# A routed four-layer transformer kernel: the router one gated step earlier, eight places for expert weights, and the last one-hots in a ring in another buffer

## The reference

```python
x = layernorm(x + lightning_attention(x))      # 4 x 512 tokens, 512 wide
x = layernorm(x + int8_ffn(x))
# gated layer
q, k, v = x@Wq.T+bq, x@Wk.T+bk, x@Wv.T+bv;  g = sigmoid(x@Wg.T+bg)
x = layernorm(x + q * cumsum(k*v, axis=1) * g)
# mixture of experts: 32 experts, inner width 192
p = softmax(x @ gate.T);  top8, idx = top_k(p, 8);  w = top8 / sum(top8)
prim, sec = idx[:, :4], idx[:, 4:]
best_sim, best = max over prim of similarity[sec, prim]
new_sec = where(best_sim < 0.5, sec, best)     # a second choice joins a first one
combine = sum(one_hot([prim, new_sec]) * w)
y = sum over experts of (silu(x@wg.T) * (x@wu.T)) @ wd.T * combine[:, e]
x = layernorm(x + y)
```

## Time and profile before

| | |
|---|---|
| median of 3 runs | 1631.88 us (1629.71 to 1634.39) |
| the profiled execution | 1634.86 us, its span 1633.0 us, granted clock 0.953 |
| PE / DVE / ACT / POOL busy | 90% / 58% / 44% / 47% |
| chain that ended last | PE 61%, DVE 12%, DMA 10%, issue 7%, POOL 6% |
| gated layer, 16 steps | 673.9 to about 868.8 us |
| tail of the router | about 868.8 to 970.3 us |
| expert blocks | 970.3 to about 1590 us |

### The profile page before, as it was taken

How to read it: one execution, slowest core, us unless ns; L and a number is a source line. 1 busy time by engine, 2 the same in 40 slices (tenths; PEclk the granted TensorE clock), 3 DMA queues, 4 the chain that set the end, 5 groups by cost and what they waited for, 6 DMA issues and landing times.

```text
span 1633.0 us, 33299 instructions
## 1 busy us (share of the span) xinstructions
PE 1462.1 (90%) x11189; PEld 825.5 (51%) x11190; DVE 944.4 (58%) x1869; ACT 724.8 (44%) x1311; POOL 770.8 (47%) x699
## 2 busy tenths in 40 slices
PE   3899999999999999999996369998988999999980
PEld 1566666644444444445553226664545666666650
DVE  6777777776757576624879664443333444444435
ACT  5344433555464546434554334443333444444443
POOL 2455554530010101233566255565555887776745
PEclk9999999999999999999997579999999999999995
DMA  6233111279677777511111058999998999888869
GB/s 234 60 122 101 29 32 33 77 246 314 225 257 229 257 234 257 180 50 52 54 54 52 2 192 222 256 277 250 268 239 242 168 169 166 152 145 143 149 94 315
DMA packets 97102, 269.52 MB, mean 165 GB/s; under 512 B 15152, under 2 KB 15568, under 8 KB 91920
## 3 DMA queue, kind: packets, MB, share of 16 engines
q1 hardware_dynamic: 61424, 182.75, 33.5%
q0 software_dynamic: 35616, 85.99, 27.0%
HBM read 158.83 MB, written 101.47 MB: 159 GB/s over the span
## 4 chain that ended last, share of the span: by engine, by line
PE 61%; DVE 12%; DMA 10%; issue 7%; POOL 6%; ACT 2%; SPq 1%; DVEq 0%; POOLq 0%; ACTq 0%
PE bank L866 15%; PE bank L546 10%; PE bank L887 8%; DMA acc<-X,WA 7%; PE bank L678 6%; PE bank L684 6%; PE bank L707 6%; PE bank L857 4%; DMA XT<-x_rows,WA 2%; DVE ARENA L1009 1%; POOL ARENA L1637 1%; POOL ARENA L1642 1%; PE bank L876 1%; ACT ARENA L1357 1%; PE bank L787 1%
## 5 line engine op out<-in xcount | busy, mean ns | idle before, releaser
L866 PE MATMUL bank<-ARENA,XT 128*128 x1908 | 367.2, 329 | 2.5 <-issue 1.4
L1768 POOL DMA_INDIRECT acc<-X,WA x159 | 252.7, 1590 | 140.7 <-DMA acc<-X,WA 65.9
L866 PEld LDWEIGHTS bank<-ARENA,XT 128*128 128x128 f16 x1908 | 181.2, 98 | 127.9 <-issue 14.8
L1321 DVE COPY XT<-bank 128x1024 f16<-128x1024 f16 x159 | 110.0, 692 | 213.0 <-PE bank L857 191.7
L887 PE MATMUL bank<-ARENA,XT 128*128 x795 | 200.2, 383 | 0.7 <-issue 0.5
L1357 ACT ACTIVATE ARENA<-ARENA 128x512 f16<-128x512 f32 (+2 forms) x128 | 89.3, 709 | 248.2 <-DVE ARENA L1093 133.3
L1762 POOL DMA_INDIRECT XT<-x_rows,WA x159 | 156.9, 987 | 83.4 <-DVE XT L1331 45.4
L1596 ACT ACTIVATE XT<-bank 128x192 f32<-128x192 f32 x159 | 52.5, 330 | 310.0 <-PE bank L866 260.9
L546 PE MATMUL bank<-WA,XT 128*128 128x512 f16 (+1 forms) x768 | 137.4, 333 | 24.1 <-DVE WA L929 19.8
L546 PE MATMUL bank<-XT,STG 128*128 128x512 f16 x640 | 150.7, 383 | 0.0
L1357 ACT ACTIVATE XT<-bank 128x384 f16<-128x384 f16 (+2 forms) x207 | 125.8, 608 | 31.7 <-PE bank L535 22.2
(11 more groups left out here) (218 smaller groups left out, 2389.0 us busy)
## 6 DMA issues: line engine op xcount, KB each, us to landing
w_scratch<-WA SPq DMA_DIRECT2D x64, 640.0 KB, 3.9
ARENA<-w_scratch SPq DMA_DIRECT2D x32, 1280.0 KB
ARENA<-w_exp SPq DMA_DIRECT2D x48, 640.0 KB, 5.3
WA<-w_exp SPq DMA_DIRECT2D x16, 640.0 KB, 5.2
ARENA<-ARENA SPq DMA_DIRECT2D x64, 128.0 KB, 2.3
acc<-ARENA SPq DMA_DIRECT2D x18, 256.0 KB, 3.0
x_rows<-ARENA SPq DMA_DIRECT2D x17, 256.0 KB, 2.4
STG<-xT SPq DMA_DIRECT2D x8, 512.0 KB, 4.3
```

What stands on the lines that cost most here:

```text
L866: mm = pe.matmul(d, xTb[k.u % 2][:, a * KD + kd, :], weights(sl, b, kd * 2 * DFF, 2 * DFF), start=(a, b, kd) == (0, 0, 0), stop=(a, b, kd) ...
L1321: dve.tensor_copy(xTb[k.u % 2].rearrange("p c n -> p (c n)"), bank[k.u % 2][:, :].bitcast(F16)).then_inc(xt_sb, 1)
L1768: pool.indirect_dma_start(acc[i % 2], bass.IndirectOffsetOnAxis(blkidx[:, i:i + 1], 0), yD[i % 8], None, compute_op=ALU.add).then_inc(y_ou ...
```

## The change

- Each router piece in the gated layer moves to an earlier place: `logits(b)` and `choices(b)` from the fourth to the third step of the batch after, `second_choices`, `similarities` and `combine` from the two steps behind that into the fourth step, `ranks` and `places` one step forward, and `slot_sums` to the end of the fourth step of batch b + 2. With this `second_choices(2)`, `similarities(2)` and `slot_sums(1)` leave the tail.
- `combine` is split: its first eight instructions are now `candidates`. In the tail `candidates(2)` runs ahead of the last residual and norms; 12 of the 32 value one-hots of batch 2 run between `choices(3)` and `candidates(3)`, and their slot sums before `ranks(3)`.
- POOL makes its row one-hots ahead of the step's product, and its `shifts` behind it for q >= 2.
- The one-hots of batches 2 and 3 lie in STG, where the weights of the gated layer were, in a ring of 19. Before, batch 2 used 32 places beside batches 0 and 1, and batch 3 a ring of 12.
- `Wslot` has eight places. The first load waits only for `slot_sums(1)`; loads 1 to 3 follow behind the rows of batch 3; places 4 to 7 lie over the gated layer's buffers and wait until these are read. From the ninth on a load waits for the expert eight before.

```diff
@@ -39,6 +39,6 @@
 NBLK = TOK * TOPK // P + EXPERTS - 1
-NSLOT = 4
+NSLOT = 8
 NG = 8
 AHEAD = 2
-NLAST = 12
+NLAST = 19
 WCOLS = KD * 2 * DFF + 2 * DIM
@@ -178,3 +178,3 @@
 
-        r = Region(ARENA, NSLOT * 4 * WCOLS)
+        r = Region(ARENA, 4 * 4 * WCOLS)
         kC, qC, gC, kvC, cumC, a1C, onesC = (r.take([SEQ], F32) for _ in range(7))
@@ -190,7 +190,7 @@
         r = Region(ARENA)
-        oneR = [[r.take([P], F16) for _ in range(ROWS_B)]] * 3
-        oneV = [[r.take([4 * P], F16) for _ in range(ROWS_B)]] * 3
-        r = Region(ARENA, NSLOT * 4 * WCOLS)
-        oneR.append([r.take([P], F16) for _ in range(NLAST)])
-        oneV.append([r.take([4 * P], F16) for _ in range(NLAST)])
+        oneR = [[r.take([P], F16) for _ in range(ROWS_B)]] * 2
+        oneV = [[r.take([4 * P], F16) for _ in range(ROWS_B)]] * 2
+        r = Region(STG)
+        oneR += [[r.take([P], F16) for _ in range(NLAST)]] * 2
+        oneV += [[r.take([4 * P], F16) for _ in range(NLAST)]] * 2
 
@@ -238,3 +238,3 @@
         yD = [X[:, j, :] for j in range(8)]
-        acc1 = Region(ARENA, NSLOT * 4 * WCOLS).take([NT, DIM], F32)
+        acc1 = Region(ARENA, (NSLOT - 1) * 4 * WCOLS - NT * DIM * 4).take([NT, DIM], F32)
 
@@ -492,13 +492,19 @@
 
-            store_rows(0)
-            store_rows(1)
-            store_weights(0)
+            for b in range(BATCH - 2):
+                store_rows(b)
+                store_weights(b)
             store_rows(2)
-            store_weights(1)
-            store_rows(3)
-            store_weights(2)
-            sp.wait_ge(onehot_used, (BATCH - 1) * TB * TOPK)
+            sp.wait_ge(onehot_used, 2 * TB * TOPK)
             load_expert(0)
+            store_weights(2)
+            store_rows(3)
+            for e in range(1, 4):
+                load_expert(e)
+            sp.wait_ge(logit_ready, BATCH)
+            for tt in range(TB):
+                sp.wait_ge(xr_out[tt], 16 * BATCH)
+            sp.wait_ge(acc_init, 16 * (3 + ROWS // P + NT))
+            load_expert(4)
             store_weights(3)
-            for e in range(1, NSLOT):
+            for e in range(5, NSLOT):
                 load_expert(e)
@@ -779,4 +785,4 @@
 
-            def slot_sums(b):
-                for i in range(ROWS_B):
+            def slot_sums(b, lo=0, hi=TB * TOPK):
+                for i in range(lo, hi):
                     n = b * ROWS_B + i
@@ -798,3 +804,3 @@
                 if et == 1 and q >= 2:
-                    similarities(q - 2)
+                    ranks(q - 2)
                 if et == 2:
@@ -804,2 +810,4 @@
                     norm_transposes(q, 2)
+                if et == 3 and q >= 1:
+                    second_choices(q - 1)
                 gate_proj(s, 2)
@@ -807,4 +815,2 @@
                     back(s - 1)
-                if et == 1 and q >= 3:
-                    slot_sums(q - 3)
                 if et == 2:
@@ -812,14 +818,11 @@
                 if et == 3 and q >= 1:
-                    logits(q - 1)
+                    similarities(q - 1)
                 gate_proj(s, 3)
-                if et == 0 and q >= 2:
-                    second_choices(q - 2)
                 if et == 1:
                     norm_transposes(q, 0)
-                if et == 2 and q >= 2:
-                    ranks(q - 2)
+                if et == 2 and q >= 1:
+                    logits(q - 1)
+                if et == 3 and q >= 2:
+                    slot_sums(q - 2)
             back(BATCH * KD - 1)
-            second_choices(2)
-            similarities(2)
-            slot_sums(1)
             for tt in range(TB):
@@ -830,2 +833,3 @@
             similarities(3)
+            slot_sums(2, 0, 12)
             ranks(3)
@@ -835,3 +839,3 @@
             pe.matmul(bank[3][0:1, 0:EXPERTS], nb[0:EXPERTS, 0:1], upper[0:EXPERTS, :], start=True, stop=True).then_inc(end_ready, 1)
-            slot_sums(2)
+            slot_sums(2, 12, ROWS_B)
             pe.wait_ge(ended_ready, 1)
@@ -1185,3 +1189,3 @@
 
-            def combine(b):
+            def candidates(b):
                 dve.wait_ge(oh_ready, b + 1)
@@ -1192,2 +1196,4 @@
                     step(dve.tensor_reduce(cand[:, :, :, j], pr, AX, ALU.add))
+
+            def combine(b):
                 step(dve.tensor_reduce(best, cand, AX, ALU.max))
@@ -1247,2 +1253,8 @@
                 q, et = s // KD, s % KD
+                if et == 1 and q >= 2:
+                    if q == 2:
+                        dve.wait_ge(d_const, 16 * 14)
+                    places(q - 2)
+                if et == 2 and q >= 2:
+                    one_hots(q - 2, ROWS_B // 2, ROWS_B)
                 running_sum(s)
@@ -1258,10 +1270,9 @@
                 if et == 1 and q >= 2:
-                    combine(q - 2)
-                if et == 2 and q >= 2:
-                    if q == 2:
-                        dve.wait_ge(d_const, 16 * 14)
-                    places(q - 2)
-                    one_hots(q - 2)
-                if et == 3 and q >= 1:
+                    one_hots(q - 2, 0, ROWS_B // 2)
+                if et == 2 and q >= 1:
                     choices(q - 1)
+                if et == 3 and q >= 1:
+                    candidates(q - 1)
+                    if q < BATCH - 1:
+                        combine(q - 1)
             residual(BATCH * KD - 1)
@@ -1271,2 +1282,4 @@
             choices(3)
+            one_hots(2, 0, 12)
+            candidates(3)
             combine(3)
@@ -1280,3 +1293,3 @@
                               ALU.mult, ALU.add).then_inc(nb_ready, 1)
-            one_hots(2)
+            one_hots(2, 12, ROWS_B)
             places(3)
@@ -1536,8 +1549,6 @@
                 act.activation(kC, bank[0][:, :], ACT.Identity, scale=1 / (WS * WS), bias=kb16[:, et:et + 1]).then_inc(kc_sb, 1)
-                if et == 1 and q >= 2:
-                    similarities_copy(q - 2)
                 if et == 3 and q >= 2:
-                    row_hots(q - 2, 0, 8)
-                if et == 0 and q >= 3:
-                    row_hots(q - 3, 16, 24)
+                    row_hots(q - 2, 8, 20)
+                if et == 3 and q >= 1:
+                    choices_copy(q - 1)
                 if et == 1:
@@ -1550,2 +1561,4 @@
                     norm_copy(q, 1)
+                    if q >= 2:
+                        row_hots(q - 2, 0, 8)
                     norm_copy(q, 2)
@@ -1557,14 +1570,9 @@
                 if et == 3 and q >= 2:
-                    row_hots(q - 2, 8, 16)
-                if et == 0 and q >= 3:
-                    row_hots(q - 3, 24, 32)
+                    row_hots(q - 2, 20, ROWS_B)
+                if et == 3 and q >= 1:
+                    similarities_copy(q - 1)
                 act.wait_ge(gc_ready, s + 1)
                 act.activation(gC, bank[5][:, :], ACT.Sigmoid, scale=1 / WS, bias=biasC[:, 3 * KD + et:3 * KD + et + 1]).then_inc(gc_sb, 1)
-                if et == 0 and q >= 2:
-                    choices_copy(q - 2)
-                if et == 3 and q >= 1:
+                if et == 2 and q >= 1:
                     exponentials(q - 1)
-            row_hots(1, 16, 32)
-            choices_copy(2)
-            similarities_copy(2)
             for tt in range(TB):
@@ -1735,3 +1743,3 @@
                 q, et = s // KD, s % KD
-                if et == 0:
+                if et == 0 and q < 2:
                     for tt in range(TB):
@@ -1745,7 +1753,10 @@
                         x_low(n0 + q * TB + tt, (n0 + q * TB + tt) % NT, hl4[tt])
-                product(s)
-                if et == 3 and q >= 2:
+                if et == 2 and q >= 2:
                     row_hots(q - 2, 0, 16)
-                if et == 0 and q >= 3:
-                    row_hots(q - 3, 16, ROWS_B)
+                if et == 3 and q >= 2:
+                    row_hots(q - 2, 16, ROWS_B)
+                product(s)
+                if et == 0 and q >= 2:
+                    for tt in range(TB):
+                        shifts(n0 + q * TB + tt, tt)
             for tt in range(TB):
@@ -1754,3 +1765,2 @@
                 x_low(n0 + BATCH * TB + tt, NT - TB + tt, hl4[tt])
-            row_hots(1, 16, ROWS_B)
             row_hots(2, 0, ROWS_B)
```

More of the change, by code:

```diff
@@ L491, in store_weights @@
                 sp.dma_start(cwcols[:, b * TB:(b + 1) * TB], comb[b % 2].bitcast(I32)).then_inc(cw_out[b % 2], 16)
-            store_rows(0)
-            store_rows(1)
-            store_weights(0)
+            for b in range(BATCH - 2):
+                store_rows(b)
+                store_weights(b)
             store_rows(2)
-            store_weights(1)
+            sp.wait_ge(onehot_used, 2 * TB * TOPK)
+            load_expert(0)
+            store_weights(2)
             store_rows(3)
-            store_weights(2)
-            sp.wait_ge(onehot_used, (BATCH - 1) * TB * TOPK)
-            load_expert(0)
+            for e in range(1, 4):
[5 more added lines that the diff above has]
+            load_expert(4)
             store_weights(3)
```

(26 more changed lines are left out.)

## The result

The changed kernel takes 1620.81 us (median of 6 runs, 1612.77 to 1624.51), the kernel before 1631.72 in the same comparison: a ratio of 0.9944, 95% interval 0.9921 to 0.9966. The quotient of the two medians is 0.9933, inside that interval. The forecast was 1610, a gain of 21.6; by the medians the gain is 10.9, and 1620.8 lies at the upper edge of the forecast range (1597 to 1621). The profiled execution took 1623.95 us, its span is 1622.1 and its clock 0.957.

A forecast was written before the change was run, and what follows sets the result against it. PE was taken to bound most of the run, DVE-led small steps the tail, transfers the loaded expert stage. Tail 14.7 plus loads 6.9 gave 21.6 us off 1631.88, so 1610.3, range 1597 to 1621.

The forecast's parts named there:

- DVE becomes the bound of the gated layer, lengthened by POOL: Gated layer, rival at 8%: DVE's burst makes PE wait 2 to 3 us per batch; tail gains 8; 1619 us.
- `places` (4.0): Gated layer: `places` takes DVE 4.0 us in the second step of the batch.
- so I book nothing more: Gated layer: POOL's work beside DVE's choices could cost some 2 us per batch; nothing was added for it.
- it is level again about 1 us before the next logits: Gated layer: DVE, late into the batch's second step, catches up about 1 us before the next logits.
- the common access would make the sum 5 us smaller: Gated layer: by the skill's page, the port pair DVE and POOL share would make the total gain 5 us smaller.
- end of the logits of batch 2: End of step 14, the point the tail is counted from: booked at 856.6 us.
- from there to `places(2)`: Tail: 37.1 us from the end of batch 2's logits, so `places(2)` starts at 893.7, 11.2 us earlier than before.
- The hole at the slot sums (-4.6): Gated layer: PE's wait at batch 0's slot sums and the half clock behind it go, 4.6 us.
- Second choices (0.3 us each): Gated layer: PE waits some 0.3 us for them in each of three batches; 0.6 booked, bounds 0 and 2 each.
- Cover for the running sum: Gated layer: the sum comes 7 us late, but PE asks for it later, with 1 to 4 us to spare.
- The split (3.5) and the ring (0): Tail: 12 of batch 2's value one-hots fill a DVE wait, 3.5 us less; the ring of 19 costs nothing.
- Loads (6.9, bounds 0 and 21): Expert stage: the last load comes 4 loads earlier, the loaded stretch is 40.6 us shorter, 6.9 us gained.

The follow-up runs named there:

- e3: The changed kernel with POOL's subtractions in the gated layer replaced by a memset that reads no buffer, leaving the low halves out of the computation; 1613.1 us.
- e4: The changed kernel with DVE's choices put ahead of the second 16 value one-hots of the batch before; 1614.3 us.
- e5: As e4, with the running sum and the residual also put ahead of `places`; 1608.0 us.
- e8: As e5, with all 32 value one-hots and slot sums of batch 2 in one piece at the old place; 1617.5 us.
- e1: The kernel before with the early loads, eight weight places and the ring of 19, every engine's router order as before; 1629.4 us.
- e6: As e5, with four places for expert weights instead of eight; 1612.7 us.
- e7: The same kernel as e5, measured again; 1608.1 us.
- e2: The changed kernel with its router order kept but four places for expert weights instead of eight; 1626.4 us.

## Why the prediction was wrong

The mechanism was right in the tail and the loads, and the size failed in the gated layer: the rival "DVE becomes the bound of the gated layer, lengthened by POOL" (1619, given 8%) is what happened. That its number is so near is luck: it had PE wait 2 to 3 us per batch, and the waits are 5.4 and 6.0.

**The step that failed** is "`places` (4.0)" together with "so I book nothing more". POOL's cost to DVE was put at nothing. Measured, it is 4.65 us per batch in `places`, which took 8.65, and 2.6 and 2.2 us in the value one-hots, against the 1 us that DVE was to have in hand. The prediction saw that POOL lengthens DVE's instructions, but weighed it only for the choices and the big compare, where one wait costs little of a long instruction. `places` was moved under POOL's four subtractions and is in the main a chain of short instructions; five of them wait for one POOL instruction each: 5 x about 0.9 = 4.6 us. The trace of before had the hint: `places(1)` there ran beside POOL's two products, and the instruction that ended with the second had 0.65 where the others had 0.18. It was plainer in `combine`, beside the very subtractions of the earlier trace rows:

```profile
841.21 1.19 DVE L1194 TENSOR_TENSOR WA<-WA 128x64 f32<-128x64 f32 x1
842.43 1.03 DVE L1195 TENSOR_SCALAR WA<-WA 128x16 f32<-128x16 f32 x1
```

The next ones, with the subtractions over, took 0.19. The prediction took from this place only L1191, a long instruction. Its own aside, that the common access would make the sum 5 us smaller, had the right sign and was not booked. The Trainium skill's rule ("SBUF — State Buffer", section "SBUF: two separate sides") that the holder keeps the port pair for a whole instruction agrees with these rows, and with e3's, where the first two short instructions end with the second and the third fill of 0.5 us.

With that, "it is level again about 1 us before the next logits" fell: DVE came 3.7 and 4.3 us after them. `places` is not the whole of it. In e3, with `places` at 4.9 us, DVE is still 2.6 and 3.7 us late, and R is 5.3 us longer than booked. What remains is the length of DVE's list ahead of the choices, the stretched one-hots in it, and e4 shows the way out: with the second 16 one-hots behind the choices the waits are 0.3 us, though `places` is as long as in the changed kernel.

In the router R was to fall by 14.7 and fell by 2.8. The missing 11.9, by the prediction's own marks (each after its first projection):
- end of the logits of batch 2: 6.2 late. Waits of 2.15, 3.29 and 2.16, 1.1 of half clock, less the 0.6 booked and 1.4 since the slot sums of batch 0 took 2.29 instead of 3.67, make 6.7, 0.5 too many.
- from there to `places(2)` (904.70): 41.95 us instead of 37.1, 4.9 more. The last wait is 3.5 above its 0.3, and half clock behind it 2.2; the 0.8 that these are too many I did not trace.
- from there on: 60.7 us against 63.4 before, 2.7 gained of 3.5.

In e5, with the waits gone, the same three come out 1.1, 1.6 and 0.0 us better than booked: R falls by 17.4.

**The hole at the slot sums (-4.6)**: right; it is gone.

**Second choices (0.3 us each)**: right in kind (e4, e5: 0.29 to 0.30 at batches 1 and 2, when DVE is free) and wrong in the changed order.

**Cover for the running sum**: wrong. The prediction said that PE "asks for it only at the k and v projections one step on", with 1 to 4 us to spare; `places` ahead of it, twice as long, used them up by 2.15.

**The split (3.5) and the ring (0)**: right; e8 gives 3.5 for the split, and e1 and e8 the 3.8 to 3.9 that the ring costs without it.

**Loads (6.9, bounds 0 and 21)**: right as far as it can be told; 8.0 in the changed kernel's E, 8.4 over all profiles, 4.6 by the medians of e6 and e7. Blocks end at 212 matmuls of L891 in 180 us instead of 205, and as before at 220 in 160 once the loads are over.

**The two halves** are worth 3 us (e1) and 6 (e2), each against the 1632.4 of its own comparison, by themselves and 10.9 together. One reason is that e1 lacks the split that hides its ring, 3.8 us. With that the halves would make 12.7, more than the whole; the difference was not traced.

## What to carry to other kernels

Before a chain of short VectorE instructions is moved, look at what GpSimd does in its new place: here five steps of 0.18 us each waited for one GpSimd instruction and lost 4.6 us together, more than any large one. The trace of before showed such waits where the two engines already ran side by side. Where an engine's list is written by hand, put first what another engine waits for soonest (here the running sum, then the choices) and the one-hots, which nobody needs for a whole step, last: that reordering alone gave 12.8 us by the medians, more than the change it was applied to. And count a wait of TensorE with the half clock behind it: it cost 1.1 to 2.2 us behind each of the four waits of 3.2 to 3.9 us at these places (after, e2, e3).

## What was not expected of the hardware

- A GpSimd instruction that reads no buffer also delays VectorE: beside fills of 0.50 us (e3) two `tensor_scalar` instructions on 32 elements took 0.82 and 0.47 us, then 0.19.
- Fp16 one-hots of 128 and 256 elements took 0.30 to 0.35 us each beside GpSimd's row one-hots and products (after, e3), against 0.23 and 0.26 in before, where GpSimd was idle.
- Waits of 2.15 to 2.17 us of TensorE for the running sum were followed four times by full speed (2.33 us for ten matmuls: both in after, the second in e2 and in e4) and twice by half (4.02, the first in e2 and in e4). What decides it was not settled; it moves R by 1.7 us.
